# A decoder layer on one core: who inverts the softmax sums of the last attention

## The chip, the cores and the metric

The kernel runs on one core of a Trainium2 chip. The metric is the device time of one execution in microseconds (us). TensorE (PE in the profile) does the matrix products, VectorE (DVE) and ScalarE (ACT) read and write both PSUM and SBUF, GpSimd (POOL) works on SBUF alone, and SyncE (SP) issues most transfers. Each engine takes its own instructions strictly in program order and waits on semaphores.

## The reference

A batch of 8 sequences of 512 tokens with 256 channels goes through three sublayers, each on a layer-normalized input and added to the residual: causal self-attention with 16 heads, cross-attention with 16 heads, and a block that is itself an attention followed by a mixture of experts. The change touches the attention of the third:

```
nx = rmsnorm(X, g1)
Q = nx @ Wq.T                      # 4 heads of 64
Kc, Vc = nx @ Wkc.T, nx @ Wvc.T    # one key and value head of 64 for all four
attn = softmax(Q Kc^T / 8)         # 512 x 512 a head
X = X + (attn @ Vc) @ Wo.T
...                                # rmsnorm, router with top 2 of 8, shared expert, experts
```

The softmax is not normalized before it meets the values. The kernel sums the exponentials by a matrix product with ones, inverts the sums and multiplies the attention's output by them.

## The kernel before, in words

The third sublayer's attention, router and shared expert are in `moe_attention`. It goes through the 8 sequences ("batches") `b` one by one, with all steps of neighbouring batches interleaved. Each engine has a list of steps, and a table `PLACE` gives each step a due time; `side_by_side` merges the steps of all batches by the due time plus `b` times `TURN` (46 us) into one fixed order for each engine. The table decides only the order: an engine that comes to a step whose data is late waits there, and all that stands behind it on this engine waits too. Between two turns the same order repeats.

A batch has two pairs of heads. For each pair the steps that matter here are these, with their names in `PLACE`:

- S and AV: TensorE makes the scores in `pS`, ScalarE the exponentials `PR` (L2202), TensorE the weighted values in `pv` (L2069).
- AD: GpSimd adds the exponentials of two blocks of keys (L2451). PU: TensorE multiplies the sums by ones into the PSUM bank `pu` (L2079), twice for pair 0 (PU0, PU1) and twice for pair 1 (PU2, PU3). Both pairs use the one bank `pu`, so PU2 must wait until the sums of pair 0 have been read: `exp_sums` waits on `s_ln` for that.
- PC: ScalarE copies the values of pair 0 out of `pv` to `Y` (L2208).
- NORM on ScalarE: `RS = Ln(pu)` (L2215), then `RS = Exp(-RS)` (L2217). NORM on VectorE: `Y = Y * RS` for pair 0 (L2294), `Y = pv * RS` for pair 1 (L2298). There is one tile `RS`.
- YS: ScalarE rounds `Y` to f16 (L2221), GpSimd takes the rest (L2457). WO: TensorE multiplies by the output weights (L2105).

Other steps stand beside these on the same engines. What stands directly behind VectorE's NORM of pair 0 is step N4, `h_n_lo` (L1805), the low halves of the normalized input of the batch two turns on; TensorE transposes it (step XT, L83, tile `f_pf`) ahead of PU3. Ahead of and behind VectorE's NORM of pair 1 stand the two `f_Q_lo` (step QK, L2277); TensorE's product for V (step V, L1999) waits for the second of them. Step MX is the row maxima (L2038 on TensorE, L2286 on VectorE), H1 and H3 the shared expert's hidden layer (L2113, L2238, L2392, L2398), TB the steps of a routing table that VectorE builds once, in the last batch's turn.

Of the kernel before, what the change touches and what calls it, by code (L numbers as in the profile page):

```python
# [11 lines left out]
ACT = mybir.ActivationFunctionType  # L12
# [12 lines left out]
def after(eng, sem, n):  # L25

    if n > 0:
        eng.wait_ge(sem, n)


class Names:
# [5 lines left out]
    def sb(self, name, shape, dt):  # L37
        return self.mem.enter_context(self.nc.sbuf_tensor(f"{self.prefix}_{name}", shape, dt))

    def ps(self, name):  # L40
        return self.mem.enter_context(self.nc.psum_tensor(f"{self.prefix}_{name}", [P, T], F32))

    def sem(self, name):
        return self.keep.enter_context(self.nc.semaphore(f"{self.prefix}_{name}"))
# [1799 lines left out]
def moe_attention(nc, keep, mem, k, x_res, d, B, groups, shared, head):  # L1844
# [7 lines left out]
    sb, ps, sem = names.sb, names.ps, names.sem  # L1852
# [40 lines left out]
    RS = sb("RS", [P, T], F32)  # L1893
# [17 lines left out]
    pv, pu = ps("pv"), ps("pu")  # L1911
# [3 lines left out]
    s_xe = sem("xe")  # L1915
    s_qk, s_hi, s_lo, s_v, s_vo = sem("qk"), sem("hi"), sem("lo"), sem("v"), sem("v_out")
    s_mx, s_red, s_nt, s_ne, s_nd = sem("mx"), sem("red"), sem("nm_turned"), sem("nm_out"), sem("nm_placed")
    s_s, s_e, s_av, s_ln, s_rc, s_y = sem("scores"), sem("exp"), sem("av"), sem("ln"), sem("recip"), sem("y")
    s_ad, s_pu, s_pc = sem("exp_added"), sem("exp_sums"), sem("pair_copied")
    s_yh, s_yl, s_wo, s_x1 = sem("yhi"), sem("ylo"), sem("wo"), sem("x1")  # L1920
    s_sq, s_ms, s_r2, s_fhi, s_flo, s_xr = (sem(n) for n in ("squares", "ms", "rms2", "fhi", "flo", "xres"))
# [15 lines left out]
    def group_end(b):  # L1937
# [15 lines left out]
        ("ACT", "S"): (60.41, 63.24, 68.15, 73.53, 77.11, 81.3, 83.76, 84.97), ("ACT", "PC"): (78.08,), ("ACT", "NORM"): (84.83, 97.35),  # L1953
        ("ACT", "YS"): (91.66, 103.51), ("ACT", "F1"): (116.25,), ("ACT", "F3"): (119.92,), ("ACT", "H1"): (139.86, 149.38),
        ("ACT", "H3"): (153.12, 159.41), ("ACT", "R1"): (151.56,), ("ACT", "R3"): (171.64,), ("ACT", "SPLIT"): (20.41, -8.45),
        ("DVE", "N1"): (-41.2,), ("DVE", "N4"): (-0,), ("DVE", "XT"): (2.76, 3.53), ("DVE", "QK"): (7.89, 9.94, 13.41),
# [12 lines left out]
    def at(engine, step, b, i=0):  # L1969
        if step == "SPLIT":  # L1970
            return at_split(engine, b)
        if step == "TB":
            return b * TURN + PLACE["DVE", "RK"][0] + 0.1 + GAP * i
        if step in ("TL", "LD"):
            return (groups[1].first - 1) * TURN + PLACE["DVE", "RK"][0] + GAP * Tables.STEPS + (0.01 if step == "TL" else 1.0)
        return b * TURN + PLACE[engine, step][i]
# [13 lines left out]
    def half(side):  # L1990
        return slice(side * D, (side + 1) * D)

    def tensor_program(eng):
# [78 lines left out]
        def exp_sums(b, j):  # L2072
            eng.wait_ge(s_ad, 4 * b + j + 1)
            if j == 0:
                after(eng, s_x1, 2 * b)
            elif j == 2:
                eng.wait_ge(s_ln, 2 * b + 1)
            for side in range(2):
                m = eng.matmul(pu[half(side), :], ones32[:, :], PR[:, 2 * j % 4, side, :], start=(j % 2 == 0), stop=(j % 2 == 1))  # L2079
            m.then_inc(s_pu, 1)  # L2080
# [92 lines left out]
    def scalar_program(eng):  # L2173
        def norm(b):
            yield at("ACT", "N4", b)
            head.normal_high(eng, b)

        def front(b):
            for c in range(3):
                yield at("ACT", "QK", b, c)  # L2180
                eng.wait_ge(s_qk, 3 * b + c + 1)
                if c == 0:
                    after(eng, s_s, 16 * (b - 1))
                out = Q[0][:, b % 2, c, :] if c < 2 else K[0][:, b % 2, :]
                eng.activation(out, pf[c % 2][:, :], ACT.Copy, scale=1 / WS).then_inc(s_hi, 1)
            yield at("ACT", "V", b)
            eng.wait_ge(s_v, b + 1)
            after(eng, s_av, 8 * (b - 1))
            eng.activation(V[:, b % 2, :, :], pf[1][:, 0:TT * D].rearrange("p (t d) -> p t d", t=TT), ACT.Copy,
                           scale=1 / WS).then_inc(s_vo, 1)  # L2190
            yield at("ACT", "NM", b)
            eng.wait_ge(s_nt, b + 1)
            after(eng, s_nd, 32 * b)
            eng.activation(NMT[:, :], pf[0][0:16, 0:P], ACT.Copy).then_inc(s_ne, 1)

        def exponentials(b):
            for i in range(8):
                yield at("ACT", "S", b, i)
                for side in range(2):
                    eng.wait_ge(s_s, 16 * b + 2 * i + side + 1)  # L2200
                    after(eng, s_pu, 4 * b + i // 2 - 1)
                    eng.activation(PR[:, i % 4, side, :], pS[side][:, :], ACT.Exp, scale=SCALE).then_inc(s_e, 1)  # L2202

        def values(b):
            yield at("ACT", "PC", b)
            eng.wait_ge(s_av, 8 * b + TT)
            after(eng, s_yl, 2 * b)
            eng.activation(Y[:, 0, :], pv[:, :], ACT.Copy).then_inc(s_pc, 1)  # L2208

        def sums(b):  # L2210
            for pair in range(2):
                yield at("ACT", "NORM", b, pair)
                eng.wait_ge(s_pu, 4 * b + 2 * (pair + 1))
                after(eng, s_y, 2 * b + pair)
                eng.activation(RS[:, :], pu[:, :], ACT.Ln).then_inc(s_ln, 1)  # L2215
                eng.wait_ge(s_ln, 2 * b + pair + 1)
                eng.activation(RS[:, :], RS[:, :], ACT.Exp, scale=-1.0).then_inc(s_rc, 1)  # L2217
                yield at("ACT", "YS", b, pair)
                eng.wait_ge(s_y, 2 * b + pair + 1)
                after(eng, s_wo, 2 * b)  # L2220
                eng.activation(YT[0][:, pair, :], Y[:, pair, :], ACT.Copy).then_inc(s_yh, 1)  # L2221

        def back(b):
            yield at("ACT", "F1", b)
            eng.wait_ge(s_x1, 2 * b + 2)
            after(eng, s_ms, b)
            for t in range(TT):
                eng.activation(sq[:, t, :], X[b % 3][:, t, :], ACT.Square, accum_out=ssq[:, t:t + 1]).then_inc(s_sq, 1)
            yield at("ACT", "F3", b)
            eng.wait_ge(s_r2, b + 1)  # L2230
            after(eng, s_sent[b % 2], 128 * (b // 2))
            for t in range(TT):
                eng.activation(N2[:, b % 2, t, 0:C], X[b % 3][:, t, :], ACT.Copy, scale=r2[:, t:t + 1]).then_inc(s_fhi, 1)
            for c in range(CK):
                yield at("ACT", "H1", b, c)
                eng.wait_ge(s_h1, 2 * b + c + 1)
                after(eng, s_hlo, 2 * b)
                eng.activation(TH[:, c, :], pb[1 - c][:, :], ACT.Tanh, scale=0.5 / WS).then_inc(s_th, 1)  # L2238
            for c in range(CK):
                yield at("ACT", "H3", b, c)  # L2240
                eng.wait_ge(s_hh, 2 * b + c + 1)
                after(eng, s_o, 2 * b)
                eng.activation(H16[0][:, c, :], TH[:, c, :], ACT.Copy).then_inc(s_hhi, 1)

        def route(b):
            yield at("ACT", "R1", b)
            eng.wait_ge(s_rx, 2 * b + 1)
            eng.activation(E[:, :, :], L[:, :, :], ACT.Exp).then_inc(s_re, 1)
            yield at("ACT", "R3", b)
            eng.wait_ge(s_rx, 2 * b + 2)  # L2250
            eng.activation(G[:, :], M[:, :], ACT.Exp).then_inc(s_re, 1)

        def splits():
            for n in range(ATT, NW):
                yield at("ACT", "SPLIT", n)
                weights.high(eng, n)

        side_by_side(over(back), over(route), over(sums), over(values), over(exponentials), over(front), over(norm, 1), splits())

    def vector_program(eng):  # L2260
# [27 lines left out]
        def sums(b):  # L2288
            for pair in range(2):
                yield at("DVE", "NORM", b, pair)  # L2290
                eng.wait_ge(s_rc, 2 * b + pair + 1)
                if pair == 0:
                    eng.wait_ge(s_pc, b + 1)
                    eng.tensor_tensor(Y[:, 0, :], Y[:, 0, :], RS[:, :], ALU.mult).then_inc(s_y, 1)  # L2294
                else:
                    eng.wait_ge(s_av, 8 * (b + 1))
                    after(eng, s_yl, 2 * b)
                    eng.tensor_tensor(Y[:, 1, :], pv[:, :], RS[:, :], ALU.mult).then_inc(s_y, 1)  # L2298
            for h in range(2):
                yield at("DVE", "WO", b, h)  # L2300
                eng.wait_ge(s_wo, 2 * b + h + 1)
                xr = X[b % 3][:, 2 * h:2 * h + 2, :]
                eng.scalar_tensor_tensor(out=xr, in0=(pv, pu)[h][:, :].rearrange("p (t c) -> p t c", t=2), scalar=1 / WS,
                                         in1=xr, op0=ALU.mult, op1=ALU.add).then_inc(s_x1, 1)
# [631 lines left out]
```

## Time and profile before

| | us |
|---|---|
| median of 3 runs | 2024.26 |
| the three runs | 2017.98, 2028.06, 2024.26 |
| the profiled execution, its own time | 2017.57 |
| its span, from the first instruction to the last | 2015.7 |

The profile is of one execution. The changed steps run from about 1435 us (the first Ln) to 1747 us (the last f16 copy of `Y`) of its span. "Busy" is the time in which an engine's datapath works on an instruction; an instruction that is held up in its midst is busy all along.

### The profile page before, as it was taken

The numbers are of one execution on the slowest core, as the hardware profiler recorded it, in microseconds if no ns is written. First come the engines' busy times: TensorE is split into PE (matmuls) and PEld (weight loads), VectorE is DVE, ScalarE is ACT, GpSimd is POOL, SyncE is SP. The second block draws the span as 40 slices with busy tenths as digits, with TensorE's granted clock in tenths as the row PEclk, the third lists the DMA queues.
The fourth block names the chain that finished last, engine by engine and source line by source line (L and its number), as shares of the span: only waits on it lengthen the run. The fifth ranks groups of instructions, "written<-read, shape, count | busy, mean of one in ns | idle before, by whom it ended". The sixth has DMA issues, their size and how long they took to land. (4 is left out here: it accounts for less than half of the span.)

```text
span 2015.7 us, 40889 instructions
## 1 busy us (share of the span) xinstructions
PE 1816.9 (90%) x13992; PEld 969.0 (48%) x13992; DVE 1407.5 (70%) x3320; ACT 1293.2 (64%) x2477; POOL 1097.1 (54%) x1102
## 2 busy tenths in 40 slices
PE   4899999999999999978999999986999999779994
PEld 2456666666666665552333333322334343346663
DVE  5666666666656566537878787784689888757777
ACT  2677776767667777636777777783566666525552
POOL 2466666666656666543443334313467776646664
PEclk8999999999999999989999999997999999989998
DMA  6233232323322232143321333201001110124466
GB/s 186 76 71 70 57 70 54 70 56 67 71 64 64 64 74 64 43 80 64 58 37 41 59 64 64 54 16 37 22 22 43 43 43 32 64 81 126 124 197 207
DMA packets 102523, 141.00 MB, mean 70 GB/s; under 512 B 16400, under 2 KB 66352, under 8 KB 102320
## 3 DMA queue, kind: packets, MB, share of 16 engines
q1 hardware_dynamic: 95408, 119.44, 25.2%
q0 software_dynamic: 6912, 18.95, 2.6%
q8 instruction: 116, 1.90, 0.4%
q14 instruction: 87, 0.71, 0.1%
HBM read 53.77 MB, written 33.90 MB: 43 GB/s over the span
## 5 line engine op out<-in xcount | busy, mean ns | idle before, releaser
L771 POOL TENSOR_TENSOR a_P_lo<-a_PR,a_P_hi 128x384 f16<-128x384 f32 (+1 forms) x384 | 378.7, 998 | 330.8 <-ACT a_P_hi L580 249.6
L1333 DVE TENSOR_REDUCE x_NM<-x_pm 128x1 f32<-128x512 f32 x512 | 341.9, 687 | 94.3 <-PE x_pm L1069 92.1
L1254 ACT ACTIVATE x_PR<-x_pS 128x512 f32<-128x512 f32 x512 | 300.8, 601 | 108.2 <-PE x_pS L1085 102.0
L700 DVE CUSTOM_DVE_ANT_0 a_pm<-a_pm,a_causal 128x128 f32<-128x128 f32 (+3 forms) x512 | 251.9, 497 | 140.5 <-PE a_pm L463 131.1
L577 ACT ACTIVATE a_PR<-a_pS 128x384 f32<-128x384 f32 (+1 forms) x384 | 202.3, 527 | 97.5 <-PE a_pS L486 79.8
L580 ACT ACTIVATE a_P_hi<-a_pS 128x384 f16<-128x384 f32 (+1 forms) x384 | 202.1, 526 | 43.5 <-PE a_pa L500 43.5
L710 DVE TENSOR_TENSOR a_Y<-a_pa,a_RS 64x512 f32<-64x512 f32 x128 | 88.0, 688 | 136.0 <-ACT a_RS L593 134.0
L463 PE MATMUL a_pm<-a_KA,a_QA 128*128 128x128 f16 (+3 forms) x512 | 148.5, 302 | 29.1 <-DVE a_NM L700 20.8
L1097 PE MATMUL x_pa<-x_PR,x_V 128*32 128x256 f32 x2048 | 166.4, 398 | 1.6
L484 PE MATMUL a_pS<-a_QA,a_KA 128*128 128x512 f16 (+3 forms) x512 | 152.2, 300 | 11.0 <-DMA a_QB<-a_NMT 5.5
L500 PE MATMUL a_pa<-a_P_hi,a_V_hi 128*128 128x512 f16 (+3 forms) x512 | 151.9, 299 | 3.7 <-POOL a_P_lo L771 3.2
L500 PE MATMUL a_pa<-a_P_hi,a_V_lo 128*128 128x512 f16 (+3 forms) x512 | 153.2, 299 | 0.0
L485 PE MATMUL a_pS<-a_QB,a_KB 128*128 128x512 f16 (+3 forms) x512 | 147.0, 300 | 0.0
L500 PE MATMUL a_pa<-a_P_lo,a_V_hi 128*128 128x512 f16 (+3 forms) x512 | 146.5, 299 | 0.0
L1408 POOL TENSOR_TENSOR x_res<-x_res,x_OT 128x256 f32<-128x256 f32 x32 | 23.5, 733 | 221.7 <-DVE x_OT L1342 221.7
L2654 PE MATMUL e_pH<-m_w_hi,e_xt 128*128 x320 | 109.8, 382 | 2.1 <-ACT e_xt L2704 1.2
L1085 PE MATMUL x_pS<-x_QT,x_KT 49*128 49x512 f16 x256 | 95.2, 390 | 12.8 <-ACT x_PR L1254 11.0
L486 PE MATMUL a_pS<-mask_kq,idb 128*128 128x128 bf16 x512 | 105.7, 219 | 0.0
L1069 PE MATMUL x_pm<-first_keys,first_queries 48*128 48x512 f16 x256 | 98.1, 398 | 8.2 <-DVE x_NM L1333 4.2
L1085 PE MATMUL x_pS<-first_queries,first_keys 49*128 49x512 f16 x256 | 95.8, 388 | 9.7 <-ACT x_PR L1254 6.9
L379 PE MATMUL a_pp<-a_xT_hi,first_keys 128*128 128x512 f16 x256 | 98.3, 384 | 3.4 <-DVE a_xT_lo L654 3.2
L2286 DVE TENSOR_REDUCE f_NM<-f_pf 128x1 f32<-128x512 f32 x128 | 82.1, 682 | 27.1 <-PE f_pf L2038 26.2
(411 smaller groups left out, 5003.9 us busy)
## 6 DMA issues: line engine op xcount, KB each, us to landing
a_QA<-a_nat_q_hi SPq DMA_DIRECT2D x128, 128.0 KB, 2.3
first_keys<-sent SPq DMA_DIRECT2D x80, 129.0 KB
a_QB<-a_nat_q_lo SPq DMA_DIRECT2D x64, 128.0 KB, 2.4
a_KA<-a_nat_k_hi SPq DMA_DIRECT2D x64, 128.0 KB, 2.4
a_KA<-a_nat_k_lo SPq DMA_DIRECT2D x64, 128.0 KB, 2.4
a_KB<-a_nat_k_hi SPq DMA_DIRECT2D x64, 128.0 KB, 2.4
e_ga<-back SPq DMA_DIRECT2D x16, 512.0 KB
first_keys<-in_w SPq DMA_DIRECT2D x12, 512.0 KB
```

The lines of the kernel that those rows point to most:

```text
L463: eng.matmul(pm[i % 2][:, 0:(t + 1) * P], QA[:, u % RQ, side, pair, t * P:(t + 1) * P], KA[:, par, side, pair, 0:(t + 1) * P], start=True, ...
L484: eng.matmul(o, KA[:, par, side, pair, ks], QA[:, u % RQ, side, pair, qs], start=True, stop=False)
L485: eng.matmul(o, KB[:, par, side, pair, ks], QB[:, u % RQ, side, pair, qs], start=False, stop=False)
L500: m = eng.matmul(pa[j % 2][:, P * kc:T], V[v][:, u % 2, kc, j, :], P16[p][:, i % RH, a:a + T - P * kc], start=(kc == 0 and n == 0), stop=( ...
L577: eng.activation(PR[:, m % RF, 0:n], pS[i % 2][:, 0:n], ACT.Exp, scale=SCALE).then_inc(s_e, 1)
L580: eng.activation(P16[0][:, m % RH, 0:n], pS[i % 2][:, 0:n], ACT.Exp, scale=SCALE).then_inc(s_eh, 1)
L700: eng.tensor_tensor_reduce(out=pm[i % 2][:, 0:n], in0=pm[i % 2][:, 0:n], in1=causal[:, T - n:T], scale=1.0, scalar=NEG, op0=ALU.add, op1=A ...
L771: eng.tensor_tensor(P16[1][:, m % RH, 0:n], PR[:, m % RF, 0:n], P16[0][:, m % RH, 0:n], ALU.subtract).then_inc(s_el, 1)
L1085: eng.matmul(pS[i % 2][:, :], KT[par][r, pair, kc * P:(kc + 1) * P], QT[par][r, pair, :], start=True, stop=True).then_inc(s_s, 1)
L1097: m = eng.matmul(pa[2 * D * j:2 * D * (j + 1), q], V[:, b % 2, kc, GH * g + j, :], PR[:, kc, j, q], start=(kc == 0 and half == 0), stop=(k ...
L1254: eng.activation(PR[:, kc, j, :], pS[i % 2][:, :], ACT.Exp, scale=SCALE).then_inc(s_e, 1)
L1333: eng.tensor_reduce(NM[:, v % 2, c:c + 1], ring_bank("max", v, n)[:, :], AX.X, ALU.max, negate=True).then_inc(s_red, 1)
```

## The change

ScalarE's two activations for each pair go away, with the semaphore between them. VectorE computes `RS = reciprocal(pu)` itself, at its own NORM step, directly ahead of the multiplication that uses it. The wait for the ones product moves to VectorE with it. PU2, which waited until Ln had read the bank, now waits for the reciprocal. The order of all other steps is as before.

```diff
@@ tensor_program, exp_sums
             elif j == 2:
-                eng.wait_ge(s_ln, 2 * b + 1)
+                eng.wait_ge(s_rc, 2 * b + 1)
@@ scalar_program, sums
         def sums(b):
             for pair in range(2):
-                yield at("ACT", "NORM", b, pair)
-                eng.wait_ge(s_pu, 4 * b + 2 * (pair + 1))
-                after(eng, s_y, 2 * b + pair)
-                eng.activation(RS[:, :], pu[:, :], ACT.Ln).then_inc(s_ln, 1)
-                eng.wait_ge(s_ln, 2 * b + pair + 1)
-                eng.activation(RS[:, :], RS[:, :], ACT.Exp, scale=-1.0).then_inc(s_rc, 1)
                 yield at("ACT", "YS", b, pair)
@@ vector_program, sums
             for pair in range(2):
                 yield at("DVE", "NORM", b, pair)
+                eng.wait_ge(s_pu, 4 * b + 2 * (pair + 1))
+                after(eng, s_y, 2 * b + pair)
+                eng.reciprocal(RS[:, :], pu[:, :]).then_inc(s_rc, 1)
                 eng.wait_ge(s_rc, 2 * b + pair + 1)
```

## Rows read from the trace of the kernel before

**Rows 1.** The page: busy time of each engine, and VectorE's 40 slices.

```profile
PE 1816.9 (90%) x13992; PEld 969.0 (48%) x13992; DVE 1407.5 (70%) x3320; ACT 1293.2 (64%) x2477; POOL 1097.1 (54%) x1102
...
DVE  5666666666656566537878787784689888757777
```

**Rows 2.** Two turns: length, busy PE PEld DVE ACT POOL, granted clock, DMA.

```profile
1522.90:1567.10 44.20, 41.54 (x308) 17.83 (x307) 41.65 (x86) 29.32 (x57) 35.02 (x29) 1.00 0.15 49
1567.10:1614.60 47.50, 44.45 (x308) 18.84 (x307) 39.30 (x85) 28.89 (x57) 34.88 (x29) 0.93 0.14 45
```

**Rows 3.** Groups by line, 1420 to 1800 us: the inversion, the multiplications, N4.

```profile
L2215 ACT ACT_TABLE_LOAD x13 | 16.7, 1283 | 0.2
L2217 ACT ACT_TABLE_LOAD x13 | 16.7, 1283 | 0.2
L1805 DVE SCALAR_TENSOR_TENSOR h_n_lo<-first_queries,h_r,h_n_hi 128x256 f16<-128x256 f32 x16 | 16.5, 1090 | 0.0
L2294 DVE TENSOR_TENSOR f_Y<-f_Y,f_RS 128x512 f32<-128x512 f32 x8 | 13.0, 1624 | 0.2 <-ACT f_RS L2217 0.2
L2217 ACT ACTIVATE f_RS<-f_RS 128x512 f32<-128x512 f32 x16 | 10.1, 630 | 0.2
...
L2215 ACT ACTIVATE f_RS<-f_pu 128x512 f32<-128x512 f32 x16 | 9.6, 598 | 21.0 <-PE f_pu L2079 17.7 <-issue 3.1
...
L1805 DVE SCALAR_TENSOR_TENSOR h_n_lo<-h_X,h_r,h_n_hi 128x256 f16<-128x256 f32 x8 | 5.1, 697 | 0.0
```

**Rows 4.** VectorE's groups by shape, whole span: reciprocals and plain passes.

```profile
L2286 DVE TENSOR_REDUCE f_NM<-f_pf 128x1 f32<-128x512 f32 x128 | 82.1, 682 | 27.1 <-PE f_pf L2038 26.2 <-issue 0.3
...
L1339 DVE RECIPROCAL x_RC<-x_pp 128x16 f32<-128x16 f32 x32 | 7.9, 248 | 17.8 <-PE x_pp L1113 17.8
...
L2324 DVE RECIPROCAL f_R<-f_R 128x4 f32<-128x4 f32 x8 | 1.4, 178 | 0.3
L2366 DVE TENSOR_TENSOR m_base<-f_pb,m_base 128x8 f32<-128x8 f32 x8 | 1.2, 151 | 0.0
```

**Rows 5.** Timeline of VectorE (start, duration) around both NORM steps.

```profile
1522.88 0.79 DVE L2294 TENSOR_TENSOR f_Y<-f_Y,f_RS 128x512 f32<-128x512 f32 x1
1523.60 4.66 DVE L1805 SCALAR_TENSOR_TENSOR h_n_lo<-first_queries,h_r,h_n_hi 128x256 f16<-128x256 f32 x4
...
1535.91 0.68 DVE L2277 SCALAR_TENSOR_TENSOR f_Q_lo<-f_pf,f_Q_hi 128x512 f16<-128x512 f32 x1
...
1567.06 3.12 DVE L2294 TENSOR_TENSOR f_Y<-f_Y,f_RS 128x512 f32<-128x512 f32 x1
1570.11 2.56 DVE L1805 SCALAR_TENSOR_TENSOR h_n_lo<-h_X,h_r,h_n_hi 128x256 f16<-128x256 f32 x4
...
1581.85 0.69 DVE L2277 SCALAR_TENSOR_TENSOR f_Q_lo<-f_pf,f_Q_hi 128x512 f16<-128x512 f32 x1
...
1703.78 1.89 DVE L2294 TENSOR_TENSOR f_Y<-f_Y,f_RS 128x512 f32<-128x512 f32 x1
...
1710.70 0.69 DVE L2298 TENSOR_TENSOR f_Y<-f_pv,f_RS 128x512 f32<-128x512 f32 x1 [3.17 <-ACT f_RS L2217]
```

**Rows 6.** Timeline of TensorE around the same steps.

```profile
1537.43 0.19 PE L1999 MATMUL f_pf<-h_wkv_hi,f_xT_hi 128*128 128x64 f16 x1
...
1568.37 1.08 PE L2079 MATMUL f_pu<-f_PR,f_ones 128*64 128x512 f32 x4
...
1572.72 1.03 PE L83 MATMUL f_pf<-id,h_n_lo 128*128 128x128 f16 x8 [2.72 <-DVE h_n_lo L1805]
1573.69 1.98 PE L2079 MATMUL f_pu<-f_PR,f_ones 128*64 128x512 f32 x4
...
1584.69 0.19 PE L1999 MATMUL f_pf<-h_wkv_hi,f_xT_hi 128*128 128x64 f16 x1
```

**Rows 7.** Waits of 1420 to 1760 us (total, times, longest): TensorE's on others.

```profile
PE f_pf L83 <- DVE h_n_lo L1805: 15.3, 6, 3.0
...
PEld f_pS L2056 <- ACT f_PR L2202: 11.6, 19, 0.8
```

**Rows 8.** Timeline of GpSimd beside VectorE's pair-0 step.

```profile
1564.98 4.65 POOL L2451 TENSOR_TENSOR f_PR<-f_PR 128x1024 f32<-128x1024 f32 x2
```

More of the change, by code:

```diff
@@ L1917, in moe_attention @@
     s_mx, s_red, s_nt, s_ne, s_nd = sem("mx"), sem("red"), sem("nm_turned"), sem("nm_out"), sem("nm_placed")
-    s_s, s_e, s_av, s_ln, s_rc, s_y = sem("scores"), sem("exp"), sem("av"), sem("ln"), sem("recip"), sem("y")
+    s_s, s_e, s_av, s_rc, s_y = sem("scores"), sem("exp"), sem("av"), sem("recip"), sem("y")
     s_ad, s_pu, s_pc = sem("exp_added"), sem("exp_sums"), sem("pair_copied")
@@ L1952, in moe_attention @@
         ("ACT", "N4"): (-1.73,), ("ACT", "QK"): (7.73, 9.93, 13.41), ("ACT", "V"): (13.72,), ("ACT", "NM"): (45.27,),
-        ("ACT", "S"): (60.41, 63.24, 68.15, 73.53, 77.11, 81.3, 83.76, 84.97), ("ACT", "PC"): (78.08,), ("ACT", "NORM"): (84.83, 97.35),
[1 row of a table added]
         ("ACT", "YS"): (91.66, 103.51), ("ACT", "F1"): (116.25,), ("ACT", "F3"): (119.92,), ("ACT", "H1"): (139.86, 149.38),
```

1 row of the table PLACE is left out of this document.

## The prediction, as put on record before the changed kernel ran

> **What bounds the kernel now.** I read the page first. TensorE is busy for 90% of the span. VectorE's slices stand at 8 or 9 from the 30th to the 34th, which is the changed stage and its fullest stretch of the whole kernel [rows 1]. The stretches say it turn by turn: in a turn of 44.2 us TensorE is busy for 41.5 and VectorE for 41.7, in the next 44.5 and 39.3 of 47.5, while ScalarE has 29 [rows 2]. So the change takes work from the engine with the most room and gives it to one with 2.5 to 8 us of room a turn. TensorE sets the pace, and what counts is where it waits for VectorE. The waits name one such place above all: in six turns it stood 15.3 us in all in front of its transposes of `h_n_lo` [rows 7]. That instruction is directly behind the pair-0 multiplication on VectorE, where the new reciprocal goes. The timeline of one turn shows the chain: multiplication from 1567.06, `h_n_lo` from 1570.11, TensorE idle for 2.72 until 1572.72 [rows 5, 6].
>
> **ScalarE's part, removed.** An inversion is Ln 0.60 and Exp 0.63, and in 13 of 16 cases a table load of 1.28 ahead of each: 3.8 us. All in all 16.7 + 16.7 + 9.6 + 10.1 = 53 us leave ScalarE [rows 3]. The worth is what TensorE waited for it. In the timelines only one turn shows it at length: in that of the seventh batch VectorE's pair-1 multiplication waits 3.17 us for the inverse [rows 5]. In the others ScalarE finishes before VectorE arrives: 0.2 us is all that the eight pair-0 multiplications waited [rows 3]. The exponentials behind the inversion come earlier, but TensorE's weight loads stood 19 times for 0.6 us each, 11.6 us, before scores until an exponential was done [rows 7]; these are mostly the alternation of two score banks, and I count nothing for it, with 0 to 11.6 us as the bounds of the gain. On the loads, the Trainium skill (ScalarE: Activation LUTs, What ACT_TABLE_LOAD costs) puts a switch at 1283 ns and about 1380 ns more of draining. The rows agree on 1283; by the page ScalarE would be relieved of more, and the sum would stay the same, since its work is hidden either way.
>
> **The reciprocal's price.** No row has one of 512 elements. Of 4 elements it takes 178 ns, of 16 it takes 248, while a plain pass over 8 takes 151 [rows 4]. The slope is (248 - 178) / 12 = 5.8 ns an element; a plain pass over 512 takes 682, a slope of (682 - 151) / 504 = 1.05. With a fixed part of 150 to 155 the 16-element row gives 5.9 to 6.1 an element. That makes 178 + 508 x 5.8 = 3.1 us to 150 + 512 x 6.1 = 3.3 us. Bounds from rows: 0.69, if the small rows hide a pass at full rate behind a larger fixed part, and 3.5. I take 3.3. The Trainium skill (VectorE: DVE Perf Modes, First, the fixed hardware budget) says that the reciprocal is an iterative divide with a repeat count of 8. Read as eight cycles an element at the page's 0.96 GHz that is an estimate of 4.4 us; the 16-element row, 97 ns over the 151 of a plain 8-element pass, speaks for six. By the page the sum below would be some 13 us more; whether by page or row, it speaks against this change. A plain pass that follows another starts 0.08 before its end; I leave that out.
>
> **Pair 0.** VectorE's multiplication of 128x512 takes 0.69 alone, but reads two SBUF operands, and where GpSimd adds the exponentials (4.65 us for two adds from 1564.98 [rows 8]) it lasts until GpSimd is through: 3.12. In turns where the multiplication escapes, `h_n_lo` behind it is stretched in its place, 0.79 and then 4.66 against 2.56 [rows 5]. The reciprocal reads PSUM and, as the small rows beside GpSimd's work keep their 178 [rows 4], should not be held. So it fills time in which VectorE was stuck. Before: multiplication plus `h_n_lo` in the first six turns is 13.0, less 1.89 for the seventh batch [rows 5] and an undisturbed 0.69 for the eighth, plus 16.5 + 5.1 [rows 3]: 32.0 us, or 5.3 a turn. After: 3.3 + 0.6 + 2.56 = 6.5. The delay of `h_n_lo`, and with it of TensorE, is 1.1 a turn, 6.7 us in six turns. Bounds: an undisturbed `h_n_lo`, four plain passes of 256 elements at 151 + 248 x 1.05 = 411 ns or 1.65 us [rows 4], gives 0.2 a turn; a reciprocal that hides nothing gives 3.3. PU2 gets a new wait: it started at 1568.37 [rows 6], and the reciprocal ends at 1567.06 + 3.3 = 1570.4. Behind it on TensorE stand the transposes of the high halves and then those of the low ones, which wait until after 1573 anyway; 2.0 us of wait, 1.0 of PU2 and 0.6 of transposes fit in front. So this wait costs nothing as long as `h_n_lo` is later; if that cover went, it would cost 2.0.
>
> **Pair 1.** Here GpSimd's adds are over and the 3.3 us come on top: the second `f_Q_lo` is done 3.3 later, and behind it the hidden layer's passes, `f_K_lo` and the maxima. TensorE's V product is first to need it. In the turn of 1567 that pass ended at 1582.54 and V began at 1584.69 [rows 5, 6], a slack of 2.15; three other turns have 2.0 to 2.15. The cost is 3.3 less the slack, 1.1 to 1.3. In the turn of 1522 the pass ended at 1536.59 and V began at 1537.43, slack 0.84, cost 2.5 [rows 5, 6]; the first turn has 0.7, cost 2.6. Six turns: 4 x 1.2 + 2.5 + 2.6 = 9.9; since V's own wait also delays what VectorE waits for, its backlog is then gone, and the maxima are late by no more than V. `s_pu` costs nothing here: PU3 is over five us before VectorE arrives.
>
> **The last two batches.** In the seventh no `h_n_lo` follows, and the inverse of pair 1 was late by ScalarE (the 3.17). After: reciprocal 0 from 1703.8 to 1707.1, PU2 and PU3 until 1709.1, reciprocal 1 until 1712.4, multiplication from there, against 1710.70 [rows 5]; TensorE is later by about 2. In the eighth the pair-0 one again falls into GpSimd's adds, under which the table's steps were held, and the pair-1 one stands bare ahead of a hidden-layer pass for which TensorE already waits: 3.3.
>
> **The sum.** 6.7 + 9.9 + 2 + 3.3 = 21.9 us. Against the execution's own 2017.57 that is 2039.5; this execution lies 6.7 under the median of the three, and on the median the forecast is 2024.26 + 21.9 = 2046.
>
> **TensorE's clock.** Behind the 2.72 wait the product PU3 took 1.98 for what took 1.08 before it [rows 6], the lower level (1.2 of 2.4 GHz); the turn's granted clock is 0.93 against 1.00 in the turn before, whose wait was 2.49, and it is 3.3 us longer [rows 2]. So some waits are followed by slow products and others, hardly shorter, are not. After the change the wait is in two parts (2.0 before PU2, about 1.5 before the low halves), and V adds one of 1 to 2.5. I take no change; bounds are -2.5 in the three turns that are slow now, and +2.5 in five more.
>
> **Rivals.**
> *It is faster.* The reciprocal streams: 0.69 us. Then pair 0 is swallowed whole, pair 1 fits into V's slack, and the seventh batch's 3.17 wait and up to 11.6 us before scores are given back: minus 1.5 to 13, middle 2017. It needs the 248 of the strided 16-element read from PSUM to be a fixed part; the 178 of an SBUF read with 4 elements speaks against that. The point at which it decides is V's slack: below 2 us it costs nothing in four of six turns.
> *It is hidden.* Price 3.1, an undisturbed `h_n_lo`, and half of the score waits given back: 1.3 - 1.2 + 8.7 + 4.9 - 5.8 = 8, so 2032, within 0.5%.
> *VectorE or the clock becomes the bound.* A turn of 44.2 had 2.55 us without VectorE's work [rows 2]; 6.6 more, less some 3 of time in which it was held, leaves none. If in three turns nothing of pair 0 is hidden (+2.2 each) and the clock falls in four more (+2.5), it is 22 + 17 = 39: 2063.
>
> **Chances.** My forecast (2037 to 2055) 0.60; VectorE or clock 0.20; hidden 0.14; faster 0.06, of which nearly all is by over 0.5%. About 0.5%, 10 us, is what a measurement of this kernel can tell. Faster by more 0.05, within 0.13, slower 0.82. The range of 2029 to 2066 leaves out the faster case, a little of the hidden one and the worst of the third.
>
> **What would show it.** RECIPROCAL on VectorE 128x512, 16 times, near 3.3 us; no table loads but one in the stage, and ScalarE 53 us less busy; pair-0 multiplications near 0.69 in place of a mean of 1.62; a wait of about 2 us at PU2 for VectorE; a wait of 1 to 2.5 at V for `f_Q_lo`; TensorE's wait for `h_n_lo` still there but shorter; the stage some 22 us longer and the rest unchanged. I would be wrong if the reciprocal's price is not near 3.3, if GpSimd holds it up as it does the multiplication, or if the score waits were ScalarE's doing.

## The result and the profile after

The changed kernel takes 2056.48 us (median of 4 runs, 2048.48 to 2061.89). The kernel before, timed beside it on the same chip, takes 2024.7. The ratio is 1.0158, 95% interval 1.0116 to 1.0200: slower by 31.8 us, 1.6%. The forecast was 2046 with a range of 2029 to 2066.

The profiled execution took 2056.38 us with a span of 2054.4, against 2017.57 and 2015.7 before. The page of the changed kernel, busy times and VectorE's 40 slices:

```profile
PE 1835.5 (89%) x13992; PEld 973.1 (47%) x13992; DVE 1440.3 (70%) x3336; ACT 1242.1 (60%) x2419; POOL 1097.0 (53%) x1102
...
DVE  5566666666566666456777888765799999756677
```

Against [rows 1] ScalarE has 51 us less and VectorE only 33 us more. The slices from the 30th to the 34th are all at 9, where before they were at 8, 9, 8, 8, 8.

The groups by line in the changed kernel from 1420 us on, VectorE's three and ScalarE's one table load:

```profile
L2287 DVE RECIPROCAL f_RS<-f_pu 128x512 f32<-128x512 f32 x16 | 53.6, 3350 | 0.1
L1805 DVE SCALAR_TENSOR_TENSOR h_n_lo<-first_queries,h_r,h_n_hi 128x256 f16<-128x256 f32 x18 | 11.1, 678 | 0.0
L2291 DVE TENSOR_TENSOR f_Y<-f_Y,f_RS 128x512 f32<-128x512 f32 x8 | 5.5, 692 | 0.3
```

```profile
L2232 ACT ACT_TABLE_LOAD x1 | 1.3, 1283 | 0.0
```

Sixteen reciprocals of 3.35 us make 53.6. VectorE is up by only 33, since it is held less while GpSimd works. The pair-0 multiplications fell from 1624 ns to 692, together 7.5 us. The four passes of `h_n_lo` take 2.56 us in each of the six turns, where they had taken 2.55 in three and 4.66 in the other three, together 6.2 us less. The rest is spread over many small passes. Of the 26 table loads of the inversion none is left.

TensorE's waits of 1420 to 1800 us, against [rows 7] (total, times, longest):

```profile
PE f_pu L2079 <- DVE f_RS L2287: 16.8, 8, 3.1
PE f_pf L1999 <- DVE f_Q_lo L2271: 12.7, 6, 3.1
PE f_pb L2113 <- DVE f_TH L2389: 7.1, 3, 4.2
PE f_pf L83 <- DVE h_n_lo L1805: 3.0, 6, 1.5
```

The first two are new. The third had been 3.6, the fourth 15.3.

One turn of the changed kernel, TensorE (start, duration, in brackets the idle time before):

```profile
1596.39 1.96 PE L2079 MATMUL f_pu<-f_PR,f_ones 128*64 128x512 f32 x4 [2.12 <-DVE f_RS L2287]
...
1599.51 0.77 PE L83 MATMUL f_pf<-id,h_n_lo 128*128 128x128 f16 x8 [0.19 <-DVE h_n_lo L1805]
...
1611.38 0.20 PE L1999 MATMUL f_pf<-h_wkv_hi,f_xT_hi 128*128 128x64 f16 x1 [2.44 <-DVE f_Q_lo L2271]
```

and VectorE in the same turn:

```profile
1592.30 0.68 DVE L2280 TENSOR_REDUCE f_NM<-f_pf 128x1 f32<-128x512 f32 x1
1592.89 3.35 DVE L2287 RECIPROCAL f_RS<-f_pu 128x512 f32<-128x512 f32 x1
1596.28 0.69 DVE L2291 TENSOR_TENSOR f_Y<-f_Y,f_RS 128x512 f32<-128x512 f32 x1
1596.89 2.56 DVE L1805 SCALAR_TENSOR_TENSOR h_n_lo<-h_X,h_r,h_n_hi 128x256 f16<-128x256 f32 x4
...
1603.65 2.48 DVE L121 SCALAR_TENSOR_TENSOR m_w_lo<-first_keys,h_gains_ws,m_w_hi 128x1024 f16<-128x1024 f32 x2
1606.05 0.69 DVE L2271 SCALAR_TENSOR_TENSOR f_Q_lo<-f_pf,f_Q_hi 128x512 f16<-128x512 f32 x1
1606.65 3.35 DVE L2287 RECIPROCAL f_RS<-f_pu 128x512 f32<-128x512 f32 x1
1610.04 0.69 DVE L2295 TENSOR_TENSOR f_Y<-f_pv,f_RS 128x512 f32<-128x512 f32 x1
1610.64 0.68 DVE L2271 SCALAR_TENSOR_TENSOR f_Q_lo<-f_pf,f_Q_hi 128x512 f16<-128x512 f32 x1
```

Read the two together. From 1592.98, the end of the last row maximum, to 1611.32, the end of the second `f_Q_lo`, VectorE is never idle by more than a few hundredths at a time. All three of TensorE's waits of this turn lie in that stretch, and V starts 0.06 us after it. I call it the VectorE stretch: from the end of the turn's last maximum to the start of V. The rest of the turn runs from V to the next last maximum. The windows of those two parts in the changed kernel (length, busy PE PEld DVE ACT POOL, granted clock, DMA share, GB/s):

```profile
1592.98:1611.38 18.40, 13.65 (x68) 5.25 (x68) 18.19 (x28) 3.69 (x8) 11.84 (x12) 0.91 0.25 86
1611.38:1640.90 29.52, 29.44 (x240) 13.06 (x240) 27.00 (x60) 18.14 (x42) 22.82 (x17) 1.00 0.06 19
```

and of the two turns of [rows 2], cut at the same events, in the kernel before:

```profile
1522.97:1537.43 14.46, 11.97 (x68) 4.75 (x68) 14.32 (x27) 7.64 (x12) 10.70 (x11) 1.00 0.25 76
1537.43:1567.14 29.71, 29.53 (x241) 13.09 (x239) 27.30 (x59) 21.64 (x45) 24.30 (x19) 1.00 0.10 36
1567.15:1584.69 17.54, 14.82 (x68) 5.57 (x68) 15.39 (x27) 7.51 (x12) 12.76 (x13) 0.81 0.28 91
1584.69:1614.71 30.02, 29.68 (x241) 13.27 (x239) 23.97 (x58) 21.44 (x45) 22.18 (x17) 1.00 0.06 19
```

In the second part TensorE is busy throughout, and little changes. In the first, VectorE is busy for 18.19 of 18.40 us in the changed kernel. Before, it was busy for 14.32 of 14.46 in the one turn, and for 15.39 of 17.54 in the other, where slow products (granted clock 0.81) helped to set V's time. So the change adds 3.9 us to a turn of the first kind and 0.9 to one of the second. In three of the six turns of the changed kernel VectorE is idle for 0.2 us of the stretch in all. In the other three it waits once for about 0.5 us, for `f_Q_hi` from ScalarE or for TensorE's transposes.

**Where the 38.7 us of span went.** The stage, counted from the first scores (1416.0, after 1426.9) to the first transposes of the experts' part (1788.8, after 1826.9), went from 372.8 to 400.0: 27.2 us. Another 10.9 lie ahead of the first scores, where both kernels run the same code, and 0.6 behind. Those 10.9 are not the change's: a second profile of the unchanged kernel (the control below) has its first scores at 1424.4, and its stage is 372.3. The headline's 31.8 is a difference of medians, with an interval of 23.5 to 40.5 us (0.0116 and 0.0200 of 2024.7). The 27.2 lies inside.

| VectorE stretch, six turns (us) | each | sum | rest of the turn, sum |
|---|---|---|---|
| before | 12.1 16.3 14.5 17.5 15.9 14.5 | 90.8 | 172.7 |
| before, profiled again | 12.1 16.3 14.5 14.5 14.5 16.1 | 87.9 | 176.1 |
| after | 17.9 18.4 18.9 18.4 18.4 17.0 | 108.9 | 174.3 |

Both parts together rose by 19.7 us, from 263.5 to 283.2. The seventh turn (33.4 to 35.6, from one pair-0 multiplication to the next) gave 2.2, and the last batch, from the start of its NORM step of pair 0 to the end of the stage (51.6 to 56.9), gave 5.3. That is the 27.2.

### The profile page after: what moved, and what is told of

It is laid out like the page before. It is cut to its first block and busy times, and to the rows that moved or that the text cites. A ratio compares the mean times of both kernels' runs of the same rounds, so it can differ in the third digit from the quotient of the medians.

```text
span 2054.4 us, 40846 instructions
## 1 busy us (share of the span) xinstructions
PE 1835.5 (89%) x13992; PEld 973.1 (47%) x13992; DVE 1440.3 (70%) x3336; ACT 1242.1 (60%) x2419; POOL 1097.0 (53%) x1102
## 5 line engine op out<-in xcount | busy, mean ns | idle before, releaser
L580 ACT ACTIVATE a_P_hi<-a_pS 128x384 f16<-128x384 f32 (+1 forms) x384 | 202.2, 527 | 44.4 <-PE a_pa L500 44.4
L1408 POOL TENSOR_TENSOR x_res<-x_res,x_OT 128x256 f32<-128x256 f32 x32 | 23.5, 733 | 225.1 <-DVE x_OT L1342 225.1
L2202 ACT ACTIVATE f_PR<-f_pS 128x512 f32<-128x512 f32 x128 | 69.4, 596 | 64.6 <-PE f_pS L2056 62.0
```

Source lines behind the costliest of these rows:

```text
L580: eng.activation(P16[0][:, m % RH, 0:n], pS[i % 2][:, 0:n], ACT.Exp, scale=SCALE).then_inc(s_eh, 1)
```

## The experiments

Each is timed against the kernel before on the same chip. "Stage" is the length defined above, from the one profiled execution. Runs of one and the same kernel spread over 20 us and more, so a ratio's interval says more than a single time.

**The reciprocal at 16 and at 256 of 512 columns, twice and once.** The change as it is, but the reciprocal covers only a part of the tile; the rest of `RS` holds 1.0, so the outputs of those tokens are not normalized.

```diff
-                eng.reciprocal(RS[:, :], pu[:, :]).then_inc(s_rc, 1)
+                eng.reciprocal(RS[:, 0:16], pu[:, 0:16]).then_inc(s_rc, 1)    # second kernel: 0:256
...
+        eng.memset(RS[:, :], 1.0).then_inc(s_rs, 1)
+        eng.wait_ge(s_rs, 1)
```

> As the changed kernel, but each reciprocal covers 16 of the 512 columns (the rest of RS stays at 1, so the outputs are not normalized): everything of the change except the length of the reciprocal. Theory (the cost is the 3.35 us that each reciprocal holds VectorE's queue): reciprocal rows near 250 ns, no wait at PU2 above 0.5 us, none at V, and a time 2 to 12 us below the kernel before, since ScalarE's part is gone. Rival (moving the work off ScalarE is what costs, by the new wait of PU2 or by other timing): still 10 us or more above before.

> As the changed kernel, but each reciprocal covers 256 of 512 columns (the rest of RS stays at 1, so half of the outputs are not normalized). Theory: 155 + 256 x 6.25 = 1.75 us a reciprocal; V's slack of 2 us in four of six turns hides the pair-1 one, pair 0 falls into the time in which GpSimd held VectorE; 0 to 8 us above before. Rival (cost in proportion to VectorE's busy time): half of the changed kernel's loss, 16 us above before.

Measured: 16 columns 2025.86 us, ratio 1.0029 (1.0001 to 1.0058), stage 366.3. 256 columns 2022.5, ratio 1.0026 (0.9994 to 1.0057), stage 373.0. The reciprocals, by the groups of each kernel:

```profile
L2287 DVE RECIPROCAL f_RS<-f_pu 128x16 f32<-128x16 f32 x16 | 4.0, 249 | 0.1
```

```profile
L2287 DVE RECIPROCAL f_RS<-f_pu 128x256 f32<-128x256 f32 x16 | 28.0, 1750 | 0.1
```

With 3350 for 512 columns that is a straight line, 6.25 ns an element. Half the length does not cost half of the loss, which would be a ratio of 1.008: a first piece of added work is nearly free. The short one was expected to beat the kernel before and did not. Its one profile was short, its twelve runs were not, so I repeated it beside a control.

> The kernel with 16-column reciprocals once more (outputs not normalized), since its timed ratio (1.0029, 1.0001 to 1.0058) and its profile (stage 6.6 us shorter than before) disagreed. Theory (the stage is really shorter, and the ratio was the spread of what lies ahead of it): a ratio between 0.995 and 1.001 and again a stage of 364 to 370 us. Rival (without ScalarE's inversion the kernel is no faster, and the profile was a lucky one): a ratio of 1.002 to 1.005 and a stage of 372 us or more.

> The kernel before, unchanged, as a control: a ratio of 1.000 within 0.3%, and a second profile that shows how far the time ahead of the changed stage (first scores at 1416.0 us in the first profile, 1426.9 in that of the changed kernel) and the stage itself (372.8 us from the first scores to the first expert transposes) vary from run to run. Theory: ahead of the stage by 5 to 12 us, the stage itself by under 4. Rival: the stage itself varies by 10 us or more, and single profiles say nothing of a few us.

Measured: 2030.26 against 2026.69, ratio 1.0013 (0.9989 to 1.0036), stage 376.1. The control, the kernel before under another label, has 0.9992 (0.9968 to 1.0016) and a stage of 372.3. So an inversion that costs ScalarE nothing and VectorE next to nothing gains at most 0.1% by either interval. ScalarE's 51 us bought nothing that these runs can tell from zero. A gain of a few us could hide behind what the short ones cost VectorE (4.0 us, and 3.6 more in the multiplications below). The profile shows why pair 0 gives nothing back. TensorE's wait for `h_n_lo` is as before, since a short reciprocal does not outlast GpSimd's adds and the multiplication is stuck in them again (mean 2071 ns):

```profile
PE f_pf L83 <- DVE h_n_lo L1805: 15.7, 6, 3.0
```

```profile
L2291 DVE TENSOR_TENSOR f_Y<-f_Y,f_RS 128x512 f32<-128x512 f32 x8 | 16.6, 2071 | 0.3
```

The same kernel's stage was 366.3 in one profile and 376.1 in the other, so a stage of one profile tells nothing finer than about 10 us where slow products come and go.

**The change for one pair alone.** VectorE inverts the one pair's sums, ScalarE the other's by logarithm and exponential as before.

```diff
 # scalar_program, first kernel (the second has pair == 0)
+                if pair == 1:
+                    yield at("ACT", "NORM", b, pair)
...
 # vector_program, first kernel (the second has pair == 1)
+                if pair == 0:
+                    eng.wait_ge(s_pu, 4 * b + 2 * (pair + 1))
+                    after(eng, s_y, 2 * b + pair)
+                    eng.reciprocal(RS[:, :], pu[:, :]).then_inc(s_rc, 1)
```

> Pair 0 by the reciprocal on VectorE, pair 1 by Ln and Exp on ScalarE as before. Theory: TensorE exchanges 15.3 us of waiting for h_n_lo against 16.8 at PU2 and 3.0 for h_n_lo, so 4 to 9 us above before. Rival (the two waits in a row bring the slow level of the clock in every turn): 15 us or more above before, with the product after PU2's wait at 1.98 us in six turns.

> Pair 1 by the reciprocal on VectorE, pair 0 by Ln and Exp on ScalarE as before. Theory: TensorE waits about 12 us in six turns at V for the second f_Q_lo and 3 to 4 in the last batch, so 12 to 18 us above before, more than pair 0 costs, though VectorE's added work is the same. Rival (cost in proportion to added busy time): the same as the pair-0 kernel, within 3 us.

Measured: pair 0 alone 2027.23 us against 2019.6, ratio 1.0040 (1.0018 to 1.0063), about 8 us, stage 378.2. Pair 1 alone 2036.27, ratio 1.0097 (1.0058 to 1.0135), about 20 us, stage 383.0. The VectorE stretches add up to 94.9 and 103.2 us (90.8 and 87.9 in the two profiles of before, 108.9 with both pairs). With pair 0 alone TensorE waits as long for the reciprocal as with both:

```profile
PE f_pu L2079 <- DVE f_RS L2295: 16.8, 8, 3.1
```

and yet the kernel is only 8 us slower. So that wait mostly stands where the wait for `h_n_lo` stood. The dearer half is pair 1, at which GpSimd's adds are over and nothing is hidden.

The two halves do not add up inside the stage. In the six turns, both parts together, pair 0 alone costs 2.8 us (263.5 to 266.3) and pair 1 alone 10.5 (to 274.0), but both cost 19.7: 6.4 more than the sum. (Against the second profile of the kernel before it is 2.3, 10.0 and 19.2.) V's start shows why. With pair 0 alone the second `f_Q_lo` is done 0.17 to 2.15 us ahead of V in every turn, so TensorE's own work still sets V's time. With pair 1 alone V starts 0.06 behind it in all six turns. The first reciprocal uses up slack that the second then no longer has. The timed ratios (8 and 20 us, against 31.8) are too coarse to show this, and each stage is of one profile.

**The time of VectorE without the waits.** The kernel before, and ahead of each multiplication a reciprocal into a tile that nobody reads. ScalarE's part, and all semaphores, are as before.

```diff
                 eng.wait_ge(s_rc, 2 * b + pair + 1)
+                eng.reciprocal(SPARE[:, :], RS[:, :])
```

> The kernel before, in which ScalarE inverts the sums as it did and VectorE in addition makes a reciprocal of the inverse (128x512, out of SBUF) into a spare tile that nobody reads, directly ahead of both multiplications. It costs VectorE the same time at the same place, but TensorE's third ones product still waits for ScalarE alone, and nothing waits for the reciprocal itself. If the cost of the change is only that what stands behind it in VectorE's queue comes 3.3 us later, this is as slow as the changed kernel: ratio 1.013 to 1.018, the stage 394 to 402 us. If the new wait of the third ones product and the slow products behind it carry a good part, it is cheaper: ratio 1.005 to 1.010, the stage 382 to 390 us. The wait for h_n_lo should be back at 2.5 to 4 us a turn, in one piece. If the reciprocal out of SBUF is held by GpSimd's adds, it would last over 3.35 us for pair 0.

Measured: 2051.41 us against 2019.45, ratio 1.0157 (1.0129 to 1.0185), stage 398.3. This is the changed kernel's ratio of 1.0158, without its new wait, without its relief of ScalarE. The wait it has in place of PU2's (its first line of waits, and the same turn in TensorE's timeline):

```profile
PE f_pf L83 <- DVE h_n_lo L1805: 21.8, 6, 4.4
```

```profile
1593.78 1.08 PE L2080 MATMUL f_pu<-f_PR,f_ones 128*64 128x512 f32 x4
1594.79 0.62 PE L83 MATMUL f_pf<-id,h_n_hi 128*128 128x128 f16 x8
1598.88 1.03 PE L83 MATMUL f_pf<-id,h_n_lo 128*128 128x128 f16 x8 [3.48 <-DVE h_n_lo L1805]
1599.85 1.98 PE L2080 MATMUL f_pu<-f_PR,f_ones 128*64 128x512 f32 x4
...
1611.54 0.20 PE L2000 MATMUL f_pf<-h_wkv_hi,f_xT_hi 128*128 128x64 f16 x1 [0.85 <-DVE f_Q_lo L2278]
```

PU2 no longer waits, the transposes of the low halves wait 3.48 in one piece, six more products behind run slow, and V waits 0.85 in place of 2.44. V starts at 1611.54, 19.0 us after the last maximum, and the turn is 47.8 us, against 47.9 in the changed kernel. So the new wait at PU2 is not needed for the loss. Where TensorE waits inside the stretch mostly changes the split of its idle time and not the turn.

It does not leave the turn quite alone. Here VectorE itself waits in the stretch for ScalarE's copy of TensorE's product for Q, which stands behind the slow products:

```profile
1606.39 0.69 DVE L2278 SCALAR_TENSOR_TENSOR f_Q_lo<-f_pf,f_Q_hi 128x512 f16<-128x512 f32 x1 [0.81 <-ACT f_Q_hi L2186]
```

That is the 0.6 by which this stretch is longer than the changed kernel's 18.4; the rest of the turn is 0.7 shorter (28.8 against 29.5). Over the six turns the two kernels have 281.3 and 283.2 us. In the seventh turn, where VectorE also has to wait for ScalarE's inverse, the spare kernel loses 4.2 more, and in the last batch 4.2 less. The equal ratios are in part such an exchange.

**Order.** Behind VectorE's NORM of pair 0 stands `h_n_lo`, for which TensorE waits in both kernels. An earlier due time of N4 puts it ahead of NORM. This was done in the kernel before, in the changed one together with four more entries of the table, and in the changed one alone.

```diff
-        ("DVE", "N1"): (-41.2,), ("DVE", "N4"): (-0,), ...
+        ("DVE", "N1"): (-41.2,), ("DVE", "N4"): (-3.0,), ...
 # the second kernel also has: PE PU (.., 94.5, 94.6), DVE NORM (89.36, 97.75), DVE RT 135.2, DVE SPLIT (58.2, 59.5)
```

> The kernel before with one due time changed: VectorE's h_n_lo stands ahead of its pair-0 multiplication, not behind it. TensorE waited 15.3 us in six turns for it. Theory (this wait bounds the turn before the change): h_n_lo is done 1 to 2 us earlier a turn, as it then meets GpSimd's adds itself; 3 to 12 us less in all. Rival (the wait only moves to the next step): within 3 us of before.

> The changed kernel with another order: on VectorE h_n_lo and the logits ahead of the pair-0 reciprocal, the pair-1 reciprocal ahead of both f_Q_lo, the two weight splits behind them in VectorE's idle time; on TensorE PU2 and PU3 behind the transposes and the first hidden-layer product. All work and all durations are as in the changed kernel. Theory (what costs is what stands behind each reciprocal, not VectorE's busy time): waits at V for f_Q_lo under 3 us and at PU2 under 6, the time 15 to 30 us below the changed kernel, 5 below to 12 above before. Rival (VectorE's 53.6 us of added work is what costs): still 20 us or more above before.

> The changed kernel with one due time altered: VectorE's h_n_lo stands ahead of the reciprocal and the pair-0 multiplication, as in the version of the kernel before that gained 6.7 us, and all else as in the changed kernel. If the wait for h_n_lo and the third ones product's wait are what costs, the time falls 5 to 15 us below the changed kernel (2036 to 2048). If VectorE's queue itself is full between them, the waits only move: within 5 us of the changed kernel, with a longer wait of the third ones product (4 to 6 us a turn) in place of the one for h_n_lo.

Measured: in the kernel before 2018.42 against 2026.69, ratio 0.9967 (0.9944 to 0.9989), stage 364.8. The changed kernel with five entries moved 2064.19, ratio 1.0169 (1.0133 to 1.0204), stage 402.5. With N4 alone 2063.28 against 2019.45, ratio 1.0210 (1.0190 to 1.0229), stage 413.7. I expected the second to gain 15 to 30 us on the changed kernel and the third 5 to 15. Neither gained. The third has a stage 13.7 us longer than the changed kernel's, though the intervals of the two ratios just touch. Its VectorE, in a turn:

```profile
1595.32 3.91 DVE L1805 SCALAR_TENSOR_TENSOR h_n_lo<-h_X,h_r,h_n_hi 128x256 f16<-128x256 f32 x4
1599.15 3.35 DVE L2287 RECIPROCAL f_RS<-f_pu 128x512 f32<-128x512 f32 x1
...
1605.62 0.69 DVE L2266 COPY f_xT_hi<-f_pf 128x1024 f16<-128x1024 f16 x1 [1.85 <-PE f_pf L83]
```

and TensorE's wait in the same turn:

```profile
1602.64 1.97 PE L2079 MATMUL f_pu<-f_PR,f_ones 128*64 128x512 f32 x4 [5.95 <-DVE f_RS L2287]
```

Now it is `h_n_lo` that runs beside GpSimd's adds and is held (3.91 in place of 2.56), the reciprocal comes bare behind it, PU2 waits 5.95, and, because the transposes stand behind PU2, VectorE itself then waits 1.85 for them. The stretch is 21.9 us in place of 18.4. In the kernel before PU2 waits for ScalarE's logarithm alone, so the same edit holds nothing up, and it gains: the stretch is 12.9 to 13.2 us in four of six turns.

**Passes taken out of the stretch.** In each of the six turns passes for the experts' weights, 2.48 us in all, stand inside the stretch. They were moved behind V, in the changed kernel and in the kernel before with N4 ahead.

```diff
-        ("DVE", "R3"): (173.38,), ("DVE", "RK"): (173.39,), ("DVE", "SPLIT"): (51.71, 39.16),
+        ("DVE", "R3"): (173.38,), ("DVE", "RK"): (173.39,), ("DVE", "SPLIT"): (61.0, 39.16),
```

> The changed kernel with one due time altered: in the turns in which a pass for the experts' weights (m_w_lo, 2.48 us, needed much later) stands between the pair-0 multiplication and the first f_Q_lo of VectorE's queue, it now stands behind f_K_lo and two row maxima, past the point at which TensorE's product for V is let go. Nothing of the inversion is touched. If what sets the end is VectorE's unbroken queue from the last row maximum to the second f_Q_lo (18.4 us a turn in the changed kernel, with gaps of 0.2 to 0.7), that stretch is 2.3 to 2.5 us shorter wherever the pass stood in it, V's wait goes, and the kernel gains 5 to 12 us: ratio 1.009 to 1.013. If the path is the new wait of the third ones product and the slow products behind it, which stand ahead of the pass, nothing is gained: ratio 1.014 to 1.018.

> The kernel before with both reorderings: h_n_lo ahead of the pair-0 multiplication (which alone gave 0.9967), and the pass for the experts' weights behind f_K_lo. With h_n_lo ahead, the stretch from the last row maximum to V is 13.0 us in most turns; the product for V hardly waits for VectorE there, so little more should be had: ratio 0.994 to 0.998. If VectorE's queue still set the end there, 2.4 us a turn: ratio 0.989 to 0.992.

Measured: 2068.01 against 2018.05, ratio 1.0238 (1.0200 to 1.0276), and 2030.2, ratio 1.0059 (1.0036 to 1.0082). Both are misses, and slower by more than either theory allowed. In the first the stretch did get shorter, from 108.9 to 101.5 us in six turns. That is half of the 14.9 moved out of it, since VectorE now waits in it for ScalarE's `f_Q_hi`, 1.07 us in the turn shown here. But the rest of the turn grew from 29.5 to 34, and the stage from 400.0 to 415.0 (in the second from 364.8, with N4 ahead alone, to 381.8). ScalarE's timeline of the first kernel says why:

```profile
1622.43 1.15 ACT L115 ACTIVATE m_w_hi<-first_keys,h_gains_ws 128x1024 f16<-128x1024 f32 x1 [3.19 <-DMA first_keys<-in_w]
```

and TensorE's, right behind:

```profile
1626.26 0.87 PE L2056 MATMUL f_pS<-f_Q_hi,f_K_hi 64*128 64x512 f16 x2 [2.91 <-ACT f_PR L2202]
```

They free the staging buffer of the next weights. Coming some 10 us later, they start the transfer late, ScalarE waits 3.19 for the data ahead of its exponentials, and TensorE 2.91 for those. From 1420 to 1800 us ScalarE stood 18.7 us in ten such waits, and TensorE 14.4 in five for the exponentials, near the 15 that the stage grew. In the unmoved order ScalarE never waited there. So the experiment does not tell the theories apart by its time. What it shows is that V's wait fell (12.7 to 7.5 us in all) by an edit that leaves the reciprocal alone. The second of the order kernels had the same step moved by 6.5 and shows the same waits for the transfer, 7.7 us in all, so a part of its miss may be theirs.

## Why the prediction came out as it did

The direction held, and so did the reciprocal's price and the places at which TensorE waits. The sum was 21.9 us, the stage's profile shows 27.2, and the medians 31.8. That the terms simply add up did not hold, and some of the agreement is luck, as said below.

- **The reciprocal's price.** Taken 3.3, measured 3.35 from PSUM, held by nothing, for both pairs. It lies between the bounds of 0.69 and 3.5, and the rival that rested on 0.69 falls. The repeat count of 8 that the Trainium skill gives the divide (VectorE: DVE Perf Modes, First, the fixed hardware budget) had led me to an estimate of 4.4 us. The trace does not agree: 3.35.
- **ScalarE's relief at nothing.** Shown by the short reciprocal, twice: ratios of 1.0029 and 1.0013, intervals that reach from 0.9989 to 1.0058. The score waits of 11.6 us are not ScalarE's inversion: in the changed kernel, without it, they are still there (below; 10.3 us, 15 times, with the short reciprocals). That excludes the hidden case as I had priced it.

```profile
PEld f_pS L2056 <- ACT f_PR L2202: 10.7, 17, 0.8
```

- **Pair 0 fills time in which VectorE was held.** Right: 5.5 us of multiplications in place of 13.0, `h_n_lo` at 2.56 a turn. Forecast 6.7 us in six turns. The change for that pair alone costs 2.8 there and 5.4 in the stage, with about 8 (4 to 13 by its interval) in the kernel's time. So by itself the term was sized too large; its full price comes only with pair 1 beside it.
- **PU2's new wait is covered.** Forecast 2.0 and free, measured 2.12 in five turns and 3.08 in the first, and the spare reciprocal, which has no such wait, is as slow. Free is shown only to within the two intervals together, some 0.5% or 10 us, and to 1.9 us in the six turns of the two profiles.
- **V waits for the second `f_Q_lo`.** Forecast a cost of 9.9 us; pair 1 alone costs 10.5 in six turns. The waits there are 12.7 with both pairs, of it 3.1 in the first turn. The slack of some 2 us that I took for four of six turns belongs to that one profile, in which three of them had slow products: the second profile of the unchanged kernel has it in two turns and 0.7 to 0.8 in the other four. That the term fits is partly luck.
- **The seventh turn.** Forecast 2, measured 2.2.

Two terms of the sum come out larger in this profile, and by their sizes they make up the 5.3 us between 21.9 and 27.2; that the other five turns match to 0.2 is luck too, since neither of their terms is right by itself. The **first turn** was forecast at 1.1 + 2.6 = 3.7 and grew by 7.0 (37.3 to 44.4); the other five were forecast at 12.9 together and grew by 12.7. In the first turn there was almost nothing for the reciprocal to hide in. VectorE and GpSimd before, around that NORM step:

```profile
1440.30 1.43 DVE L2294 TENSOR_TENSOR f_Y<-f_Y,f_RS 128x512 f32<-128x512 f32 x1
1441.66 2.56 DVE L1805 SCALAR_TENSOR_TENSOR h_n_lo<-h_X,h_r,h_n_hi 128x256 f16<-128x256 f32 x4
```

```profile
1438.83 2.35 POOL L2451 TENSOR_TENSOR f_PR<-f_PR 128x1024 f32<-128x1024 f32 x1 [0.15 <-PE f_pv L2069]
```

GpSimd was through at 1441.18, so the multiplication lost 0.74 us and not 2.4. I took one mean for all six turns (5.3 us for the pair of instructions) and 1.1 from it. With pair 0 alone this turn's stretch grows by 2.5, with pair 1 alone by 2.7 and the rest of the turn by another 1.1, which I had as "late by no more than V". The **last batch** was forecast at 3.3, all of it for pair 1, with pair 0 counted as covered. It grew by 5.3. TensorE's waits for VectorE's hidden-layer passes there were 1.55 and 0.81 before, and are

```profile
1779.71 0.39 PE L2113 MATMUL f_pb<-f_fT_hi,m_w_hi 128*128 128x512 f16 x1 [1.55 <-DVE f_TH L2389]
1785.38 0.61 PE L2113 MATMUL f_pb<-f_fT_hi,m_w_hi 128*128 128x512 f16 x1 [4.20 <-DVE f_TH L2389]
```

after: 3.4 for pair 1, as forecast. For pair 0 VectorE reaches `f_L`, for which TensorE waits too, 6.47 us after the start of NORM in place of 4.99: a reciprocal of 3.35 hid 1.9 and cost 1.5. But these two delays, 4.9 at that point, are not what is left at the end. When TensorE starts on the router's products for the last time, 3.2 of them remain (1.7 with pair 1 alone, 1.5 with pair 0 alone). The other 2.1 arise behind that, where nothing was changed: from there to the end of the stage it is 21.4 and 20.6 us in the two profiles of the kernel before, 18.4 to 22.9 in the other kernels, and 23.6 in the changed one. With pair 1 alone the last batch takes no longer than before (51.5 us against 51.6), with pair 0 alone 0.7 longer. So how much of the 5.3 is the change's stays open.

**The clock** was taken at no change, and the turns bear that out, though for a reason that the prediction did not give. The slow products behind a wait lie in the VectorE stretch. Before, they could set V's time (the turn with a clock of 0.81 has 2.1 us of VectorE's idle time in its stretch). After, VectorE's queue covers most of them: of the four middle turns the one without slow products has a stretch of 18.4, and those with them have 18.9, 18.4 and 18.4.

**The rival of VectorE as the bound** (2063, chance 0.20) was half right. VectorE is the bound now, but for 18.4 us of a turn and not for the whole (it is busy for 45.2 of 48). In the other 29.5 us TensorE is, as before, and the two alternate. My main case had this bound in pieces, as one delay at `h_n_lo` and another at V, where one queue was the truer picture. In the sum that left out that the two pairs draw on one slack (6.4 us in six turns); for the repairs it made all the difference. I expected the reordered kernels to win back the waits that I saw, and a wait inside a stretch that another engine fills gives nothing back.

What stays open is the rest, 31.8 against 27.2. With stages of one kernel up to 10 us apart and an interval of 17 us on the difference, it is within what these measurements can tell.

The version that beats both kernels is the kernel before with `h_n_lo` ahead of the multiplication: 0.9967, though by 0.3% only. It shows too that a wait does count while the receiving engine has slack: TensorE's wait for `h_n_lo` fell from 15.3 to 6.1 us, and the six turns from 263.5 to 254.2.

## What to carry to other kernels

Find the stretch in which the receiving engine is never idle, from the last event that another engine hands it to the first that it hands back, and price moved work by what it adds between those two points, less the slack before the engine that takes over. Work beyond that slack counts in full, so two moved pieces in one stretch are priced together (2.8 and 10.5 us alone, 19.7 together, in this kernel), and waits inside a filled stretch are not terms of a sum. Where the moved instruction hides behind a hold-up, look at the hold-up turn by turn, first and last turn apart, and not at its mean. When a filler pass is moved, ask what buffer it frees: 2.48 us of passes a turn, needed by nobody soon, cost 15 to 17 us of stage where it came some 10 us later, in the main through the transfer that waits for its buffer.

## What the runs showed of the hardware

- VectorE's fp32 reciprocal out of PSUM takes 249, 1750 and 3350 ns for 16, 256 and 512 elements a partition, and 3344 out of SBUF. A plain pass of 512 takes about 0.69 us.
- GpSimd's adds over SBUF hold VectorE's passes with two SBUF operands (a multiplication 3.12 us in place of 0.69) and `h_n_lo` (4.66 and 3.91 in place of 2.56). They hold no reciprocal, not even one that reads and writes SBUF: the spare ones in the adds' time all took 3.34 or 3.35, and the multiplications behind them, which came when the adds were over, 0.63.
- The 2.56 of `h_n_lo` is itself not undisturbed. Its four passes take 1.67 where GpSimd is idle (at 1419.06 in the changed kernel). In the turns one of the four takes 1.37 in place of 0.48, beside GpSimd's pass for the low half of `Y` (1.46), which comes soon behind the multiplication.
- In the changed kernel the wait of 3.08 us at PU2 and three of the five of 2.12 were followed by a slow product (1.96 to 1.98 in place of 1.08), one by 1.36 and one by 1.08. Before, a product of 1.98 followed waits of 2.58, 2.72 and 2.97, and none followed 2.49 and 2.51.
- A table load on ScalarE took 1283 ns, and the activation behind it started 0.01 us after its end (load at 1487.16, Exp at 1488.45 in the kernel before). Behind a Tanh the pair of Ln and Exp took two loads, one ahead of each.
